# A transformer tower on one core: the last pair's end in two halves of the heads

## The chip, the core and the metric

The kernel runs on one core of a Trainium2 chip. The metric is device time in microseconds (us). PE is the matrix engine, DVE the vector engine, ACT the activation engine, POOL the general engine, and SP issues the DMAs. The five run their own streams in order and meet at semaphores.

## The reference

16 sequences of 512 tokens, 64 channels, all float32. In three steps:

```python
h = tok(ids)                                  # sines of 4 ids, two-layer MLP, layernorm, plus 0.1 * residual
h = h + attn(layernorm(h))                    # 8 heads of 64, one shared k and v; softmax; output product
h = h + ffn(layernorm(h))                     # router of 6 experts, top 2, three-layer experts
```

In the attention `ctx` of shape (b, 8, s, 64) is transposed over its heads and reshaped to (b, 512, s) before the output product with `Wo`, whose result is (b, s, 64). Written out, output token 64 h + d depends on head h alone (and on all tokens through its keys and values). So the tokens of a head can go through the last layernorm and the expert layer as soon as that head is done, whatever the others do.

## The kernel before, in words

**Pairs.** Two sequences make a pair, and there are 8 (`PAIRS`). A pair has 16 heads in all, taken two at a time (`a` = 0 to 7, `HH` = 8 such head pairs) and in quads of four (`QUADS` = 4). It is walked in 64 slots. A slot is one 128x512 tile of scores: its product on PE (L494, made for two slots at a time), its maximum on DVE (`maxima`, L899), its exponential on ACT (`exps`, L786, which also sums the row). Per 8 slots (one `a`) there are also the reciprocal of the sums (L905), the scaled output weights `woz` (`over_sums`, L349, on POOL; for the very last `a` on DVE), the product of the exponentials with them in two parts (`pv`, L525) and a block transpose into `m` on DVE (`turn`, L911). Per 16 slots one quad's queries are made (L506) and copied out (L792).

**What else runs beside the slots.** Beside pair i's scores run the token part of pair i+1 (`prep`) and the end of pair i-1 (`ffn`, `ffn_out`): the values' product FIN (`value_products`, L609), the addition to h (L1095), the layernorm (L916 to L939, with a power on POOL, L1204, and squares on ACT, L797), the transposes T (L535, copied out at L829), the router R and its logits L (L648, L659), the gating of 22 small DVE instructions in 7 parts (`gating`, L1029 to L1079), the experts E1 and E2 (L673, L684, copied out at L834, L1111 and L838), the last product Y in four blocks (L708), and the weighted sums of the outputs (L1126 on DVE, L358 to L371 on POOL).

**What sets the order.** Each engine's stream is written out by hand: for each slot the code issues the scores' instruction first and then whatever the tables say for that slot. `F` is the table for the ends of pairs 0 to 5, `Z` for pair 6 (which runs beside pair 7 and past it, slots 64 to 77) and `L` for pair 7 (after the last slot; `FIN0` is at slot 63). No queue is reordered. So a late wait on an engine holds back all that is behind it.

**The ring.** PSUM is a ring of four double banks (`RING`), and every product takes one (FIN takes two). `ring_order` lists the products in the order of PE's stream, `ring_places` gives each the bank whose last reader is earliest by the tables (`read_at`), and `free` makes PE wait for that reader.

**The last pair (table L).** FIN is in three parts (`fin_part`): FIN0 with all heads of the first sequence and the first four of the second, FIN1, and FIN2 with the two heads that come last. The rest of the end is on all 8 tiles of tokens: h, layernorm on DVE with POOL's power, 12 products of zeros (`warm`, L745) ahead of T, router, gating, E1, E2 (half of it copied by ACT), and four Y blocks, each weighted by DVE (`outputs`, L1137), with the sums in turn on POOL (even blocks) and DVE (odd blocks, L1141, L1144).

**Stores.** SP waits for the sums of a pair and stores it with two DMAs, one per sequence (L421 to L426).

## Time and profile before

| | us |
|---|---|
| median of 3 runs (705.65 to 707.96) | 707.37 |
| the profiled execution | 705.38 |
| its span, first to last instruction | 703.6 |
| PE busy | 650.5 (92%) |
| DVE busy | 546.5 (78%) |
| ACT busy | 470.0 (67%) |
| POOL busy | 277.9 (39%) |

Times below are counted from the start of the span. PE's busy time is that of the matmuls, whose ends are modelled; a row's start to the next row's start is the better price of one. In a timeline the columns are start, length, engine, line, operation, operands, count, and in brackets the idle time before it with what ended it.

### The profile page before, as it was taken

How to read it: one execution, taken by the hardware profiler on the slowest of the kernel's cores; microseconds unless marked ns; L12 is line 12 of the kernel's file. 1: busy time of each engine (PE TensorE's matmuls, PEld its weight loads, DVE VectorE, ACT ScalarE, POOL GpSimd, SP SyncE). 2: the span in 40 equal slices, each digit the busy share in tenths (PEclk: the TensorE clock that was granted, in tenths of full speed). 3: DMA queues.
4: the chain of work that ended last, by engine and by line, in shares of the span. 5: the costliest groups of instructions: out<-in, count | busy, mean ns of one | idle time of the engine just before them, and what ended most of it. 6: DMA issues, size and time to landing. Idle time of an engine off the chain costs nothing.

```text
span 703.6 us, 26738 instructions
## 1 busy us (share of the span) xinstructions
PE 650.5 (92%) x11632; PEld 370.6 (53%) x11632; DVE 546.5 (78%) x1078; ACT 470.0 (67%) x1183; POOL 277.9 (39%) x354
## 2 busy tenths in 40 slices
PE   5789999999999999999999999999999999999974
PEld 4445555445645465545654465454664446554652
DVE  5687878787797877878787887978878788687657
ACT  2678885975668665886658766687558866678321
POOL 1242215315652175502853146620764119211173
PEclk9899999999999999999999999999999999999999
DMA  4000000000000000000000000000000000000001
GB/s 164 1 3 3 1 3 3 3 2 2 18 2 2 2 3 18 2 2 2 17 5 2 2 3 18 2 2 2 3 18 2 2 2 3 18 2 3 3 2 32
DMA packets 9428, 6.66 MB, mean 9 GB/s; under 512 B 8672, under 2 KB 8800, under 8 KB 9184
## 3 DMA queue, kind: packets, MB, share of 16 engines
q1 hardware_dynamic: 9312, 4.97, 2.4%
q8 instruction: 91, 1.49, 0.9%
q14 instruction: 25, 0.20, 0.1%
HBM read 2.87 MB, written 2.10 MB: 7 GB/s over the span
## 4 chain that ended last, share of the span: by engine, by line
PE 60%; DVE 22%; ACT 7%; issue 6%; POOL 4%; DMA 0%; SPq 0%; DVEq 0%; ACTq 0%; POOLq 0%
PE s_bank L525 23%; PE s_bank L494 17%; DVE nmax L899 8%; ACT p L786 5%; PE s_bank L609 5%; DVE e2t L1111 3%; PE s_bank L684 3%; PE s_bank L673 2%; PE s_bank L506 2%; DVE st L916 2%; PE s_bank L708 1%; DVE hatt L1095 1%; PE s_bank L588 1%; PE s_bank L535 1%; ACT e1t L834 1%
## 5 line engine op out<-in xcount | busy, mean ns | idle before, releaser
L786 ACT ACTIVATE p<-s_bank,nmax 128x512 f32<-128x512 f32 x512 | 347.8, 691 | 146.9 <-DVE nmax L899 145.8
L899 DVE TENSOR_REDUCE nmax<-s_bank 128x1 f32<-128x512 f32 x512 | 325.5, 681 | 50.2 <-PE s_bank L494 49.6
L494 PE MATMUL s_bank<-kf,g 64*64 64x512 f32 x2048 | 260.9, 594 | 6.4 <-DVE y L1126 2.8
L525 PE MATMUL s_bank<-p,woz 64*64 64x256 f32 x4096 | 247.1, 377 | 10.0 <-POOL woz L349 4.4
L525 PEld LDWEIGHTS s_bank<-p,woz 64*64 64x64 f32 x4096 | 163.6, 133 | 124.8 <-issue 45.9
L349 POOL TENSOR_TENSOR woz<-cst,rz 128x256 f32<-128x256 f32 x126 | 74.6, 613 | 264.0 <-DVE rz L905 264.0
L494 PEld LDWEIGHTS s_bank<-kf,g 64*64 64x64 f32 x2048 | 74.2, 133 | 91.3 <-issue 48.1
L786 ACT ACTIVATION_READ_ACCUMULATOR p<-s_bank,nmax 128x1 f32 x512 | 105.3, 206 | 0.0
L911 DVE STREAM_TRANSPOSE m<-s_bank 128x512 f32<-128x512 f32 x64 | 45.6, 712 | 26.1 <-PE s_bank L525 26.1
L1204 POOL TENSOR_TENSOR st<-st,power 128x8 f32<-128x8 f32 x24 | 39.5, 1648 | 45.3 <-DVE st L926 45.3
L358 POOL TENSOR_TENSOR y<-y,gt 128x768 f32<-128x768 f32 x28 | 41.3, 1475 | 37.9 <-DVE gt L1079 20.7
L797 ACT ACTIVATE sq<-xc 128x512 f32<-128x512 f32 x24 | 15.0, 627 | 41.9 <-DVE xc L935 26.1
L1126 DVE TENSOR_TENSOR y<-s_bank,cst 128x768 f32<-128x768 f32 x28 | 26.7, 953 | 16.6 <-PE s_bank L708 10.2
L506 PE MATMUL s_bank<-kf,qk 64*64 64x512 f32 x256 | 33.9, 595 | 4.1 <-ACT p L786 3.1
L1111 DVE TENSOR_SCALAR e2t<-s_bank,cst 128x512 f32<-128x512 f32 x45 | 31.5, 745 | 5.7 <-PE s_bank L684 5.3
L708 PEld LDWEIGHTS s_bank<-cst,e2t 64*64 64x64 f32 x1536 | 27.5, 136 | 14.1 <-issue 10.7
L708 PE MATMUL s_bank<-cst,e2t 64*64 64x64 f32 x1536 | 28.2, 220 | 6.2 <-DVE e2t L1111 6.2
L366 POOL TENSOR_TENSOR ys<-y 128x384 f32<-128x384 f32 x30 | 30.0, 1001 | 9.0 <-DVE y L1137 6.8
L609 PE MATMUL s_bank<-m,v 32*64 32x256 f32 (+2 forms) x1152 | 31.9, 355 | 0.8 <-ACT p L786 0.6
L792 ACT COPY g<-s_bank 128x1024 f32<-128x1024 f32 x31 | 31.2, 1007 | 0.0
L609 PEld LDWEIGHTS s_bank<-m,v 32*64 32x64 f32 x1152 | 25.7, 131 | 7.7 <-issue 4.1
L834 ACT ACTIVATE e1t<-s_bank,cst 128x1024 f32<-128x1024 f32 x24 | 26.9, 1122 | 4.3 <-PE s_bank L673 4.1
(117 smaller groups left out, 501.6 us busy)
## 6 DMA issues: line engine op xcount, KB each, us to landing
tower_out<-o SPq DMA_DIRECT2D x16, 128.0 KB, 2.7
cst<-consts SPq DMA_DIRECT2D x1, 1070.0 KB, 8.1
e2t<-ids SPq DMA_DIRECT2D x1, 896.0 KB, 5.4
cst<-consts SPq DMA_DIRECT2D x1, 416.0 KB, 5.9
cst<-consts SPq DMA_DIRECT2D x1, 288.0 KB, 3.6
e2t<-ids SPq DMA_DIRECT2D x1, 128.0 KB, 2.9
cst<-consts SPq DMA_DIRECT2D x1, 3.0 KB, 1.7
```

The costliest lines, as they stand in the source:

```text
L349: ops.tensor_tensor(woz[:, kept, four, :].rearrange("q (m h) c -> q m h c", h=2), k("wo").rearrange("q (m c) -> q m c", m=4)[:, 2 * n:2 * ...
L358: ops.tensor_tensor(yt, yt, gt[:, 8, two, :].unsqueeze(3).to_broadcast([128, 2, NE, C]), ALU.mult).then_inc(y_pool, 1)
L494: last = pe.matmul(double[half(q), 512 * r:512 * r + 512], g[half(r), a // 2 % 2, a % 2, first:first + 64], kf[half(r), par, a // 4, :], s ...
L506: last = pe.matmul(double[half(q), 512 * r:512 * r + 512], qk[half(r), 2 * (quad % 2) + q, :], kf[half(r), par, quad // 2, :], start=True, ...
L525: last = pe.matmul(bank("PV", i, a)[half(q), 512 * hh:512 * hh + 256], woz[half(r), kept, 2 * mm + hh, :], keys[:, q, :, :], start=(part = ...
L609: last = pe.matmul(bank("FIN", i, s2)[half(b2), 512 * q + 32 * first:512 * q + 32 * end], v[quarter(g4), par, b2, n, :], m[quarter(g4), b2 ...
L708: last = pe.matmul(double[half(q), 512 * c + C * x:512 * c + C * x + C], e2t[half(c), x, first:first + 64], k("e3")[half(c), C * x:C * x + ...
L786: nc.scalar.activation(p[:, 8 * kept + c % 8, :], bank("S", i, c - r)[:, 512 * r:512 * r + 512], ACT.Exp, bias=nmax[:, c % 16:c % 16 + 1], ...
L899: nc.vector.tensor_reduce(nmax[:, c % 16:c % 16 + 1], bank("S", i, c - r)[:, 512 * r:512 * r + 512], AX.X, ALU.max, negate=True).then_inc( ...
L911: nc.vector.transpose(m[:, b2, n:n + 2, :, :].rearrange("q h n o -> q h (n o)"), bank("PV", i, a)[:, :].rearrange("q (h x) -> q h x", h=2) ...
L1111: last = nc.vector.tensor_scalar(e2t[:, 2 * e + r, :], bank("E2", i, e)[:, 512 * r:512 * r + 512], k("e2b")[:, 2 * e + r:2 * e + r + 1], 0 ...
L1204: nc.gpsimd.tensor_tensor(st[n][:, 4, :], st[n][:, 3, :], power[:, :], ALU.pow).then_inc(ln_step[n], 1)
```

## The change

The end of pair 7 is made in two halves. Table `L` goes. `LA` is the end of the first half: the heads 0 to 3 of both sequences, tiles 0 to 3, Y blocks 0 and 1. Its slots count from slot 32 of pair 7, so that it runs beside the second half of that pair's scores (its FIN is at slot 41, its Y at slot 63, its last output at slot 24 after the end). `LB` is the second half, and its slots count from slot 64. To have heads 0 to 3 of both sequences ready by slot 40, pair 7 takes its quads in the order 0, 2, 1, 3. FIN is in three parts again: heads 0 to 3 of both sequences; heads 4 to 7 of the first and 4, 5 of the second; heads 6, 7 of the second. All of LA's and LB's instructions work on four tiles, half as wide as before, so there are twice as many of them (except FIN, Y and the outputs, whose number stays).

Table `Z` is new from slot 16 on: pair 6's E1, E2 and Y come at slots 28 to 58 and its last output at slot 60, where they were at 44 to 77. The 12 products of zeros stay only in LB. The last pair is stored in two halves of the tiles, four DMAs where there were two. In all pairs a Y block now holds two neighbouring tiles (`2 * j, 2 * j + 1`, before `j, j + 4`), and x2 and the logits are laid out to match; the number and the sizes of those instructions are as before.

```diff
@@ -92,45 +92,90 @@
 Z = {'FIN': 11,
  'LN': 11,
  'SQ': 15,
- 'LN2': 16,
- 'T': 22,
- 'T_ACT': 20,
- 'R': 23,
- 'R_ACT': 23,
- 'L': 24,
- 'GATE': (26, 26, 29, 31, 36, 42, 43),
- 'GATE_ACT': (25, 36),
- 'E1': (44, 47, 54),
- 'E1_ACT': (45, 47, 54),
- 'E2': (59, 62, 63),
- 'E2_DVE': (58, 64, 66),
- 'Y': (65, 72, 75, 77),
- 'Y_DVE': (69, 71, 74, 77)}
-L = {'FIN0': 63,
- 'FIN1': 0,
- 'FIN2': 9,
- 'LN': 7,
- 'SQ': 0,
- 'LN2': 8,
- 'T': 12,
- 'T_ACT': 9,
- 'R': 13,
- 'R_ACT': 9,
+ 'LN2': 18,
+ 'T': 23,
+ 'T_ACT': 23,
+ 'R': 24,
+ 'R_ACT': 24,
+ 'L': 26,
+ 'GATE': (26, 28, 28, 29, 33, 38, 41),
+ 'GATE_ACT': (25, 37),
+ 'E1': (28, 33, 38),
+ 'E1_ACT': (29, 33, 39),
+ 'E2': (34, 39, 40),
+ 'E2_DVE': (37, 39, 40),
+ 'Y': (46, 49, 52, 58),
+ 'Y_DVE': (46, 47, 53, 60)}
+LA = {'FIN': 9,
+ 'LN': 9,
+ 'SQ': 9,
+ 'LN2': 12,
+ 'T': 17,
+ 'T_ACT': 15,
+ 'R': 17,
+ 'R_ACT': 16,
+ 'L': 21,
+ 'GATE': (21, 22, 24, 24, 26, 31, 32),
+ 'GATE_ACT': (21, 28),
+ 'E1': (19, 22, 25),
+ 'E1_ACT': (19, 22, 24),
+ 'E2': (25, 26, 28),
+ 'E2_ACT': (23, 25, 27),
+ 'E2_DVE': (24, 26, 30),
+ 'Y': (31, 31),
+ 'Y_DVE': (35, 56)}
+LB = {'FIN': 9,
+ 'FIN2': 15,
+ 'LN': 11,
+ 'SQ': 9,
+ 'LN2': 19,
+ 'T': 18,
+ 'T_ACT': 18,
+ 'R': 18,
+ 'R_ACT': 26,
  'L': 28,
- 'GATE': (14, 24, 31, 31, 31, 37, 61),
- 'GATE_ACT': (18, 32),
- 'E1': (23, 42, 45),
- 'E1_ACT': (15, 19, 24),
- 'E2': (43, 50, 55),
- 'E2_ACT': (28, 39, 53),
- 'E2_DVE': (35, 35, 35),
- 'Y': (57, 60, 62, 63),
- 'Y_DVE': (61, 62, 63, 63)}
+ 'GATE': (27, 28, 29, 33, 35, 40, 57),
+ 'GATE_ACT': (28, 56),
+ 'E1': (25, 36, 38),
+ 'E1_ACT': (28, 32, 37),
+ 'E2': (39, 39, 48),
+ 'E2_ACT': (38, 54, 63),
+ 'E2_DVE': (34, 37, 39),
+ 'Y': (61, 63),
+ 'Y_DVE': (61, 63)}
+PARTS = ((LA, SLOTS // 2), (LB, SLOTS))
+def real_quad(i, quad):
+    return (0, 2, 1, 3)[quad] if i == PAIRS - 1 else quad
+def real_pair(i, a):
+    return 2 * real_quad(i, a // 2) + a % 2
+def last_parts(slot):
+    for n, (table, first) in enumerate(PARTS):
+        if 0 <= slot - first < SLOTS:
+            yield table, PAIRS - 1 + n, slot - first
+def outputs_of(f):
+    return (0, 1) if f is LA else (2, 3) if f is LB else (0, 1, 2, 3)
...
+            if i + 1 == PAIRS:
+                for table, index, own in last_parts(slot):
+                    ffn(index, own, table)
...
+    f, first = F if i + 2 < PAIRS else Z, SLOTS * (i + 1)
+    if i + 1 >= PAIRS:
+        n = e // 2 if name == "Y" else i + 1 - PAIRS
+        f, first, e = PARTS[n][0], SLOTS * (PAIRS - 1) + PARTS[n][1], e % 2 if name == "Y" else e
...
+        def part_of(f):
+            js = outputs_of(f)
+            first, end = js[0], js[-1] + 1
+            return js, slice(2 * first, 2 * end), slice(128 * first, 128 * end), len(js) == 2
...
-            yt, two = y[:, j % 2, :, :, :], slice(j, 8, 4)
+            yt, two = y[:, j % 2, :, :, :], slice(2 * j, 2 * j + 2)
...
-            def store(i, last=False):
-                sp.wait_ge(y_pool, 4 * W_SUM * i + (2 * W_LAST if last else 4 * W_SUM))
-                if last:
-                    sp.wait_ge(y_dve, 4)
+            def store(i, tiles):
                 for b2 in range(2):
                     dst = out[2 * i + b2, :, :].rearrange("(h d) c -> d h c", d=KD)
-                    sp.dma_start(dst, o[64 * b2:64 * b2 + 64, :, :]).then_inc(stored, 16)
-            for n in range(PAIRS):
-                store(n, n == PAIRS - 1)
-            sp.wait_ge(stored, 32 * PAIRS)
+                    sp.dma_start(dst[:, tiles, :], o[64 * b2:64 * b2 + 64, tiles, :]).then_inc(stored, 16)
+            for n in range(PAIRS - 1):
+                sp.wait_ge(y_pool, 4 * W_SUM * (n + 1))
+                store(n, slice(0, 8))
+            for part in range(2):
+                sp.wait_ge(y_pool, 4 * W_SUM * (PAIRS - 1) + W_LAST * (part + 1))
+                sp.wait_ge(y_dve, 2 * part + 2)
+                store(PAIRS - 1, slice(4 * part, 4 * part + 4))
+            sp.wait_ge(stored, 32 * (PAIRS + 1))
...
+                heads = real_quad(i, quad)
                 for r in range(2):
                     for q in range(2):
-                        last = pe.matmul(double[half(q), 512 * r:512 * r + 512], qk[half(r), 2 * (quad % 2) + q, :],
-                                         kf[half(r), par, quad // 2, :], start=True, stop=True)
+                        last = pe.matmul(double[half(q), 512 * r:512 * r + 512], qk[half(r), 2 * (heads % 2) + q, :],
+                                         kf[half(r), par, heads // 2, :], start=True, stop=True)
...
-                i, par = PAIRS - 1, (PAIRS - 1) % 2
-                pe.wait_ge(mtd, HH * i + HH - 2 + n)
-                if n == 0:
-                    free("FIN", i, 0)
-                    free("FIN", i, 1)
-                value_products(i, par, *(((0, 0, 8), (1, 0, 4)), ((1, 4, 6),), ((1, 6, 8),))[n]).then_inc(fin_parts, 1)
+                i, index, par = PAIRS - 1, PAIRS - 1 + min(n, 1), (PAIRS - 1) % 2
+                pe.wait_ge(mtd, HH * i + (HH // 2, HH - 1, HH)[n])
+                if n < 2:
+                    free("FIN", index, 0)
+                    free("FIN", index, 1)
+                heads = (((0, 0, 4), (1, 0, 4)), ((0, 4, 8), (1, 4, 6)), ((1, 6, 8),))[n]
+                value_products(index, par, *heads).then_inc(fin_parts, 1)
...
+                if slot == f["FIN"]:
+                    if ends:
+                        fin_part(i + 1 - PAIRS)
+                    else:
+                        pe.wait_ge(mtd, HH * i + HH)
+                        free("FIN", i, 0)
+                        free("FIN", i, 1)
+                        value_products(i, par, (0, 0, HEADS), (1, 0, HEADS)).then_inc(fin_ps, 1)
+                if f is LB and slot == f["FIN2"]:
+                    fin_part(2)
...
+                    if f is LB:
                         pe.wait_ge(ln_dve[2], LN_DVE * i + 1)
                         free("XT", i)
                         warm(WARM_T, bank("XT", i))
                     pe.wait_ge(ln_step[2], LN_STEP[2] * i + 3)
...
+                                last = pe.matmul(double[half(q), 512 * r:512 * r + count],
+                                                 k("e1")[half(r), first:first + 64], xt[half(r), cols],
...
+                    if not nxt:
+                        for table, index, own in last_parts(slot):
+                            ffn(index, par, own, table)
+                            ffn_out(index, own, table)
...
+                b2, n = real_pair(i, a) // 4, 2 * (real_pair(i, a) % 4)
...
+                    wait(dve, y_pool, 4 * W_SUM * min(i, PAIRS - 1))
...
+                    if ends:
+                        dve.wait_ge(fin_parts, 1 if f is LA else 3)
...
+                pair = PAIRS - 1
                 dve.wait_ge(gated, i + 1)
-                dve.wait_ge(y_pool, 4 * W_SUM * i + (W_LAST if j == 2 else 0))
+                dve.wait_ge(y_pool, 4 * W_SUM * pair + (W_LAST if j == 2 else 0))
...
-                    dve.wait_ge(stored, 32 * i)
+                    dve.wait_ge(stored, 32 * pair)
...
-                ffn(PAIRS - 1, 1, slot, L)
+                for table, index, own in last_parts(slot + SLOTS):
+                    ffn(index, 1, own, table)
```

The rest of the diff passes `tiles`, `cols` and `count` of `part_of(f)` to the layernorm, the gating and the copies, so that they take those of their half, and calls `last_parts` in the streams of ACT, DVE and POOL as in PE's.

## Rows read from the trace of the kernel before

**Rows 1.** The page's first part: busy time and share.
```profile
PE 650.5 (92%) x11632; PEld 370.6 (53%) x11632; DVE 546.5 (78%) x1078; ACT 470.0 (67%) x1183; POOL 277.9 (39%) x354
```

**Rows 2.** Busy time by stretch: start and end, length, engines, clock, DMA.
```profile
587.40:624.30 36.90, 35.22 (x601) 20.87 (x605) 27.65 (x55) 25.34 (x69) 16.55 (x23) 1.00 0.04 10
624.30:655.50 31.20, 30.82 (x399) 15.01 (x395) 25.86 (x55) 24.66 (x65) 4.73 (x8) 1.00 0.01 2
655.50:671.60 16.10, 15.24 (x476) 10.98 (x472) 8.13 (x14) 2.37 (x8) 4.05 (x6) 1.00 0.01 3
671.60:703.60 32.00, 18.75 (x464) 11.81 (x462) 21.33 (x46) 7.31 (x11) 17.81 (x24) 0.90 0.08 18
```

**Rows 3.** PE's timeline around the last scores.
```profile
654.62 1.04 PE L494 MATMUL s_bank<-kf,g 64*64 64x512 f32 x8
...
656.34 1.91 PE L525 MATMUL s_bank<-p,woz 64*64 64x256 f32 x32
...
659.13 4.75 PE L609 MATMUL s_bank<-m,v 32*64 32x256 f32 x192
663.81 0.93 PE L708 MATMUL s_bank<-cst,e2t 64*64 64x64 f32 x48
664.56 1.04 PE L525 MATMUL s_bank<-p,woz 64*64 64x256 f32 x15
666.23 3.31 PE L525 MATMUL s_bank<-p,woz 64*64 64x256 f32 x49 [0.64 <-issue]
...
670.38 1.16 PE L609 MATMUL s_bank<-m,v 32*64 32x64 f32 x64
```

**Rows 4.** DVE's timeline, FIN and a Y block of pair 6.
```profile
601.51 0.75 DVE L1095 TENSOR_TENSOR hatt<-h,s_bank 128x256 f32<-128x256 f32 x2 [3.64 <-PE s_bank L609]
...
664.80 0.96 DVE L1126 TENSOR_TENSOR y<-s_bank,cst 128x768 f32<-128x768 f32 x1 [2.26 <-PE s_bank L708]
```

**Rows 5.** The chain that ended last: start, length, what.
```profile
671.60 1.42 DVE h L1095 x4
...
676.63 1.66 POOL st L1204
...
679.06 0.69 PE s_bank L535 x32
679.76 1.04 PE s_bank L708 x48
680.80 0.85 PE s_bank L648 x8
681.65 1.73 PE s_bank L673 x8
```

**Rows 6.** DVE's timeline: gating, outputs, end.
```profile
683.89 0.21 DVE L1029 TENSOR_REDUCE gs<-s_bank 128x8 f32<-128x48 f32 x1 [2.08 <-PE s_bank L659]
...
685.75 0.80 DVE L1043 TENSOR_TENSOR gt<-gt,gs 128x48 f32<-128x48 f32 x1
...
688.98 2.06 DVE L1111 TENSOR_SCALAR e2t<-s_bank,cst 128x512 f32<-128x512 f32 x3
...
691.08 0.17 DVE L1068 TENSOR_SCALAR gs<-gs 128x8 f32<-128x8 f32 x1
...
692.37 2.02 DVE L1137 TENSOR_TENSOR y<-s_bank,gt 128x768 f32<-128x768 f32 x2
...
699.54 0.31 DVE L1144 TENSOR_TENSOR o<-ys,h 128x128 f32<-128x128 f32 x1
```

**Rows 7.** The page's DMA issues: KB each, us to landing.
```profile
tower_out<-o SPq DMA_DIRECT2D x16, 128.0 KB, 2.7
...
cst<-consts SPq DMA_DIRECT2D x1, 3.0 KB, 1.7
```

**Rows 8.** Busy time by stretch after the transposes, for PE's clock.
```profile
679.00:681.00 2.00, 1.94 (x86) 1.78 (x90) 1.03 (x3) 0.58 (x1) 1.05 (x1) 0.73 0.03 8
681.00:683.50 2.50, 2.50 (x38) 1.13 (x32) 0.81 (x1) 0.78 (x2) 2.29 (x4) 0.53 0.00 0
```

More of the change, by code:

```diff
@@ L153, in ffn @@
     def ffn(i, slot, f):
-        if f is not L and slot == f["FIN"]:
+        if slot == f["FIN"]:
             order.extend([("FIN", i, 0), ("FIN", i, 1)])
@@ L163, in ffn @@
                 order.append(("E2", i, e))
-        for j in range(4):
-            if slot == f["Y"][j]:
-                order.append(("Y", i, j))
+        for n, j in enumerate(outputs_of(f)):
+            if slot == f["Y"][n]:
+                order.append(("Y", min(i, PAIRS - 1), j))
     for slot in range(SLOTS):
@@ L191, in ring_order @@
                 ffn(i - 1, slot, F if i + 1 < PAIRS else Z)
-            if i + 1 == PAIRS and slot == L["FIN0"]:
-                order.extend([("FIN", i, 0), ("FIN", i, 1)])
+            if i + 1 == PAIRS:
+                for table, index, own in last_parts(slot):
+                    ffn(index, own, table)
     for slot in range(SLOTS):
@@ L198, in ring_order @@
         ffn(PAIRS - 2, slot + SLOTS, Z)
-        ffn(PAIRS - 1, slot, L)
+        for table, index, own in last_parts(slot + SLOTS):
+            ffn(index, own, table)
     return order
@@ L682, in ffn @@
                             for c in range(2):
[L683 to L684 removed]
+                                first, from_col = e * 128 + 64 * r, 512 * c + cols.start
+                                last = pe.matmul(double[half(c), 512 * r:512 * r + count],
                                                  k("e2")[half(r), first:first + 64],
[L686 removed]
+                                                 e1t[half(r), e, from_col:from_col + count], start=True, stop=True)
                         last.then_inc(e2_ps, 1)
             def ffn_out(i, slot, f=F):
[L690 to L694 removed]
+                js, tiles, cols, ends = part_of(f)
+                for n, j in enumerate(js):
+                    if slot == f["Y"][n]:
+                        pair = min(i, PAIRS - 1)
+                        free("Y", pair, j)
+                        double = bank("Y", pair, j)
+                        if ends:
                             for c in range(2):
@@ L773, in _ @@
                 ffn_out(PAIRS - 2, slot + SLOTS, Z)
-                ffn(PAIRS - 1, 1, slot, L)
-                ffn_out(PAIRS - 1, slot, L)
+                for table, index, own in last_parts(slot + SLOTS):
+                    ffn(index, 1, own, table)
+                    ffn_out(index, own, table)
         @block.scalar
@@ L867, in body @@
                         ffn(i - 1, slot, F if nxt else Z)
+                    if not nxt:
+                        for table, index, own in last_parts(slot):
+                            ffn(index, own, table)
             def sines(n):
@@ L890, in _ @@
                 ffn(PAIRS - 2, slot + SLOTS, Z)
-                ffn(PAIRS - 1, slot, L)
+                for table, index, own in last_parts(slot + SLOTS):
+                    ffn(index, own, table)
         @block.vector
@@ L1116, in ffn @@
                     if slot == f["GATE"][part]:
-                        gating(i, part)
-                for j in range(4):
-                    if slot == f["Y_DVE"][j]:
-                        dve.wait_ge(y_ps, 4 * i + j + 1)
-                        src = bank("Y", i, j)[:, :].rearrange("q (t c) -> q t c", t=2)[:, :, 0:NE * C]
-                        if f is L:
+                        gating(i, part, f)
+                for n, j in enumerate(js):
+                    if slot == f["Y_DVE"][n]:
+                        pair = min(i, PAIRS - 1)
+                        dve.wait_ge(y_ps, 4 * pair + j + 1)
+                        src = bank("Y", pair, j)[:, :].rearrange("q (t c) -> q t c", t=2)[:, :, 0:NE * C]
+                        if ends:
                             outputs(i, j, src.rearrange("q t (e c) -> q t e c", e=NE))
@@ L1160, in body @@
                         ffn(i - 1, 1 - par, slot, F if nxt else Z)
+                    if not nxt:
+                        for table, index, own in last_parts(slot):
+                            ffn(index, par, own, table)
             dve.wait_ge(load_four, 16)
@@ L1188, in _ @@
                 ffn(PAIRS - 2, 0, slot + SLOTS, Z)
-                ffn(PAIRS - 1, 1, slot, L)
+                for table, index, own in last_parts(slot + SLOTS):
+                    ffn(index, 1, own, table)
         @block.gpsimd
@@ L1255, in body @@
                         ffn(i - 1, slot, F if nxt else Z)
+                    if not nxt:
+                        for table, index, own in last_parts(slot):
+                            ffn(index, own, table)
             nc.gpsimd.memset(spare[:, :], 0.0).then_inc(spare_set, 1)
@@ L1270, in _ @@
                 ffn(PAIRS - 2, slot + SLOTS, Z)
-                ffn(PAIRS - 1, slot, L, True)
+                for table, index, own in last_parts(slot + SLOTS):
+                    ffn(index, own, table)
 def laid_out(x):
```

202 lines of the change are left out of this document (95 added, 107 removed).

## The prediction

> **What bounds the kernel now.** I read the page first, then the busy time by stretch of the last pair and of what follows it, then PE's timeline at the end of the scores, DVE's timeline, and the chain that ended last. The page shows PE busy for 92% of the span [rows 1]. The stretches split the part that the change touches [rows 2]. The first half of pair 7's slots (587.4 to 624.3) has PE busy 35.2 of 36.9 us, the second half (624.3 to 655.5) 30.8 of 31.2: both are PE's, and DVE has 9.2 and 5.3 us to spare. From the end of the last scores to the end of FIN (655.5 to 671.6) PE is busy 15.2 of 16.1. In the last 32.0 us no engine is busy for more than two thirds: this is a chain of single instructions. So the change trades PE time in a full stretch against idle time in an empty one. What counts is how much more the second half of the slots takes, and by how much the two stretches behind it shrink. Three runs before have a median of 707.37; the profiled execution took 705.38 with a span of 703.6. I make the sum on the span and put the difference on the median. A measurement of this kernel can tell 0.3% (2.1 us) from no change.
>
> **Term 1: the slots get longer.** Prices on PE: 0.86 for a product like the scores' (two from 654.62 to 656.34), 0.75 for a Y block (663.81 to 664.56), 4.7 for FIN0 and FIN1 together, of which FIN1, like FIN2, is 1.1, so 3.6 for a FIN that is 256 columns wide and 1.8 for the new first part with 128 [rows 3]. In the first half of the slots one E1 of pair 6 comes in: +0.9. In the second half pair 6 loses that E1 (-0.9) and gets two E2 (+1.7) and four Y (+3.0) that lay behind the last scores; the first half of the heads brings its FIN (1.8), six halves of E1 and E2 (6 x 0.43 = 2.6), and T, R and L (about 0.9, half of what the chain has for T and R and as much again [rows 5]). Together 9.1: PE's 30.8 become 39.9.
> DVE in the same stretch: 25.9 now. Pair 6's third gating part goes ahead of it (-1.3, it ran beside POOL), two more pairs of e2t copies (4 x 0.66 = 2.6, from three in 2.06 [rows 6]) and four Y additions (4 x 0.9 = 3.6 [rows 4]) come in. From the first half of the heads come: four additions to h at 0.25 and a layernorm of about 1.8; 17 gating instructions at 0.235 (4.0); three e2t copies at 0.37 (1.1). Sum 38.7. The two engines are then as good as equally full, and each waits for the other. In the first half of the slots, where PE idles 1.7 of 36.9 (4.6%), DVE is 75% full [rows 2]; the same share of 39.9 would be 1.8 lost. With DVE at over 90% I take 2.4, and as bounds 0 and 9 (below). The stretch is 42.3 long instead of 31.2. The last scores end 0.9 + 11.1 = **12.0 us later**, at 667.5.
> ACT has 24.7 busy and gets some 6: covered. POOL gets pair 6's four sums (4 us each) and one power. They stand in front of `woz`, and the worst bunch (slots 46 to 55) is 13.2 us of POOL's against about 12 of slots, with `woz` wanted five slots later: nothing, and 1 to 2 us if the sums come later than their slots. Before, these sums lay beside an idle end.
>
> **Term 2: from the last scores to the end of FIN.** Now 16.1. After: the rest of the second-last products (1.7 [rows 3]); the first half's two Y blocks (2 x 1.4: 0.75, and 0.65 for the bias of 384 columns); the last pair of heads, 3.5 if it costs 2 x 1.73 and 5.0 as it did (664.56 to 669.54, with 0.64 of "issue") [rows 3], I take 4.2; the second FIN part 1.8, beside which DVE's last transpose is hidden; the third 1.2. Sum 11.7: **4.4 us less**. It is less because FIN0, Y of pair 6 and an E2 have gone ahead. The last reciprocal and `woz` on DVE come ahead of the first half's last gating parts in DVE's stream, so these hold up nobody but the first half's own output; that output waits for pair 6's stores too, and only POOL's sum and the second last store stand behind it.
>
> **Term 3: the last 32.0 us, on half the tiles.**
> - To the last layernorm step (671.6 to 679.06): additions to h 1.42, now 1.0 (a 128x128 addition is 0.31 [rows 6], a 128x256 one 0.36 [rows 5]); six DVE and ACT steps and the squares, 4.4 together, of which 0.2 each is fixed (0.17 for 128x8 [rows 6]) and the rest halves: 2.9; POOL's power 1.66 [rows 5]. No row has it on 4 columns: between 0.83 and 1.66, I take 1.1, nearer to the half, since 8 elements cost ten times a plain small operation.
> - T to the logits (679.06 to 683.89, 4.8): about half, 2.6. Pair 6's Y, which stood between T and R [rows 5], is gone.
> - Gating (683.89 to 692.37, 8.5): e2t 2.06 becomes 1.1; 22 instructions at 0.24 (5.2) become 4.7, for 128x48 takes 0.21 and 128x8 0.17; 1.2 over goes, which is DVE slowed while POOL made pair 6's sums (0.80 for L1043 [rows 6], whose like take 0.21); 0.4 stays for the exponential's round trip. The first half's second output (2.8, a quarter of 7.5 plus a sum) is put on DVE between the layernorm and this gating, where 2.6 is free: +0.4. Sum 6.6.
> - Outputs 692.37 to 699.85: 7.5 for four blocks, 3.75 for two.
> - Last sum to the end: 3.75. A store of 128 KB lands in 2.7, one of 3 KB in 1.7 [rows 7]; so the half lies between 2.75 and 3.75, and I take 3.6.
> Sum 21.5: **10.5 us less**, bounds 19.5 and 24.
> The Trainium skill ("DMA: Bandwidth & Descriptors", the table of two cost components) gives a DMA about 2.0 us fixed and its bytes over 436e9 per second. By that a store of 64 KB would end 0.15 before one of 128, so the last term would be 3.6 also, and the stores in halves would be worth next to nothing.
>
> **Covered.** The new places of tiles in Y, x2 and logits: same counts and sizes in every pair. The other order of quads: only indices. Two more DMAs on SP, which waits anyway: its second last pair of stores needs the first half's sums, some 15 us before the end. WARM_T remains in front of T and now ends about 0.5 us ahead of it.
>
> **Sum.** 12.0 - 4.4 - 10.5 = **-2.9**: span 700.7, and 704.5 on the median.
>
> **Rivals.**
> *DVE becomes the bound, with its waits (slower).* DVE's stream is strict, so a wait for PE holds back the maxima of the scores. Rows for such waits: 3.64 for a FIN, during which only two banks are left to the scores [rows 4]; 2.08 for logits [rows 6]; 2.26 for a Y block [rows 4], of which I take half for each of four. With 10.2 of idle on 38.7 of work the second half of the slots takes 48.9, 6.6 above my 42.3: 12.0 + 6.6 - 4.4 - 10.5 = +3.7, 711.1. It decides from 47.3 (8.6 us idle) on. For it: the two sums are equal. Against it: now DVE idles there mostly because PE is late, and some of the waits would fall into PE's share.
> *The half-sized end runs at the lower clock (no change).* After the idle time before the transposes PE's granted clock falls to 0.73 and 0.53 [rows 8], its level of 1.2 GHz, and an E1 takes 1.73 instead of 0.86 [rows 5]. The new end has shorter matmuls with gaps of their own; at that level all through, its E2 and two Y blocks cost some 2 us more: -0.9, 706.5. Against it: the idle stretch before T shrinks from 2.3 to about 0.5.
> The Trainium skill ("TensorE: Matmul & The Clock Gate", the two states) says that an idle PE falls back to 1.2 GHz until it has been kept busy; the trace agrees.
> *It all fits (more).* No loss in the slots and no gap in the last heads' product: -2.4 and -0.7 more: -6.0, 701.4. For it: the second half now loses only 0.4.
>
> **How the numbers follow.** Forecast 0.46, DVE bound 0.21, lower clock 0.18, all fits 0.15. Faster by over 0.3% is the first and the last: 0.61; the same 0.18; slower 0.21. The forecast's own range is 701.5 to 707. The whole range reaches down past "all fits" by half the bounds of term 3, to 699.5, and up to 710.0, which leaves out most of the slower rival's upper half.
>
> **What would show it.** The last score product ends near 667.5 (12 us later) and the second half of the slots lasts about 42; PE is busy 94% there, DVE over 90%. FIN ends 11.7 later, the rest takes 21.5. Slower if that half lasts over 47, with DVE idle behind FIN, logits and Y of the first half. I am wrong about the end if from FIN's end on it still takes over 24, by a power that doesn't shrink or matmuls at 1.2 GHz; wrong about POOL if PE waits for `woz` at slots 52 or 60.

## The result and the profile after

The changed kernel has a median of 704.64 us in 20 runs (702.99 to 706.34), the kernel before 707.02 in 20 runs (704.82 to 708.05). The ratio is 0.9968, with an interval of 0.9958 to 0.9978: 2.4 us faster, just above the 0.3% that the prediction set as what can be told. The forecast was 2.9 us and 704.5. One execution in one of the experiments below (12 early, second output early) took 852.06 at a granted clock of 0.75 and stays out of its ratio.

The runs of the changed kernel lie in two groups. Nine are between 703.0 and 703.7, with a mean granted clock of PE of 0.990 to 0.993; eight are between 705.4 and 706.3, with 0.986 or 0.987; three lie between. The execution that was profiled took 705.7, so it is of the upper group, and its span of 703.9 is no shorter than that of the profile before. The kernel before spreads too: five of its 20 runs are between 704.8 and 705.9, fifteen between 706.5 and 708.1, and its profiled execution (705.38) is like the five. So these two traces together show 0.3 us more where the 20 runs each show 2.4 less. The gain is told by the medians and the ratio; the traces tell what single steps cost. No trace of the lower group of the changed kernel was kept.

Busy time by stretch, of the kernel after, cut where its own last score product and its own FIN end (start:end, length, PE, PE's weight loads, DVE, ACT, POOL, granted clock, DMA):

```profile
587.91:625.19 37.28, 36.04 (x609) 20.79 (x613) 28.40 (x58) 26.10 (x69) 16.57 (x23) 1.00 0.04 10
625.19:668.71 43.52, 41.42 (x812) 22.07 (x808) 37.75 (x88) 28.48 (x75) 17.83 (x25) 1.00 0.01 3
668.71:681.34 12.63, 11.43 (x404) 8.35 (x396) 6.04 (x16) 2.74 (x9) 5.26 (x9) 1.00 0.11 25
681.34:703.90 22.56, 13.15 (x224) 9.61 (x224) 14.05 (x43) 4.58 (x11) 3.33 (x5) 0.82 0.06 13
```

Against [rows 2] the slots take 80.8 us instead of 68.1, the way to the end of FIN 12.6 instead of 16.1, and the rest 22.6 instead of 32.0. Pair 7 also begins 0.5 later (587.91 against 587.37). The change doesn't touch what lies before it; the granted clock was lower in the start-up (a mean of 0.65 instead of 0.72 from 10 to 20 us). Over all 14 traces pair 7 begins between 587.2 and 588.4, so this alone moves an execution by up to 1.2 us.

PE's timeline of the kernel after, from the last score product on (start, length, engine, line, operation, operands, count, idle time before it and what ended it), to set beside [rows 3]:

```profile
667.85 1.07 PE L550 MATMUL s_bank<-kf,g 64*64 64x512 f32 x8
668.74 1.91 PE L582 MATMUL s_bank<-p,woz 64*64 64x256 f32 x32
...
673.16 3.96 PE L582 MATMUL s_bank<-p,woz 64*64 64x256 f32 x64
677.04 2.74 PE L666 MATMUL s_bank<-m,v 32*64 32x128 f32 x178
680.85 0.45 PE L666 MATMUL s_bank<-m,v 32*64 32x64 f32 x14 [1.07 <-issue]
682.75 5.49 PE L812 MATMUL s_bank<-spare 128*128 128x128 f32 x24 [1.45 <-DVE st L992]
688.17 0.71 PE L592 MATMUL s_bank<-cst,x 64*64 64x64 f32 x16
```

Two things are new. The second and third part of FIN (together 192 matmuls) stop after 178 of them, and PE stands for 1.07 us that the profile puts on nothing ("issue"). And the 24 matmuls on zeros (12 products of `warm`) take 5.49 us, where they took 2.94 before. The transposes behind them start at 688.17. DVE had written their input by 686.0. The zeros in PE's timeline of the kernel before:

```profile
673.79 2.94 PE L745 MATMUL s_bank<-spare 128*128 128x128 f32 x24 [1.40 <-DVE st L916]
```

DVE's timeline of the kernel after, in the order of [rows 6]:

```profile
685.60 0.42 DVE L1015 TENSOR_TENSOR x<-xc,st 128x256 f32<-128x256 f32 x1 [1.13 <-POOL st L1289]
...
690.90 0.18 DVE L1106 TENSOR_REDUCE gs<-s_bank 128x4 f32<-128x24 f32 x1 [2.18 <-PE s_bank L722]
...
696.80 2.03 DVE L1218 TENSOR_TENSOR y<-s_bank,gt 128x768 f32<-128x768 f32 x2
...
700.35 0.29 DVE L1225 TENSOR_TENSOR o<-ys,h 128x128 f32<-128x128 f32 x1
```

PE's granted clock around the zeros, by stretches of 1 us of the same trace (columns as above):

```profile
681.00:682.00 1.00, 0.31 (x14) 0.17 (x10) 0.64 (x4) 0.00 (x0) 0.00 (x0) 1.00 0.00 0
682.00:683.00 1.00, 0.25 (x1) 0.25 (x2) 0.90 (x5) 0.00 (x0) 0.00 (x0) 0.54 0.06 16
683.00:684.00 1.00, 1.00 (x6) 1.00 (x7) 0.52 (x2) 0.42 (x1) 0.00 (x0) 0.50 0.00 0
...
688.00:689.00 1.00, 0.88 (x18) 0.52 (x16) 0.69 (x2) 0.05 (x1) 0.00 (x0) 0.54 0.00 0
689.00:690.00 1.00, 0.63 (x16) 0.43 (x16) 0.00 (x0) 0.43 (x2) 0.00 (x0) 1.00 0.00 0
```

After the standing in FIN and the idle time before the zeros, the clock is at 0.5, the level of 1.2 GHz, and stays there until the zeros are over. They were put there to lift the clock. They ran at half of it, nearly twice as long as planned, and held back what they should have helped. That is 2.2 us (688.17 less 686.0), and the two groups of runs are some 2.5 apart. That this is what parts the groups is likely, not shown. There are also states between: in two kernels below with the same zeros at the same place (the last pair stored whole, and three parts all behind the transpose) the clock came back up while the zeros ran; they took 4.57, and the transposes started 1.2 us after their input was there.

```profile
682.69 4.57 PE L811 MATMUL s_bank<-spare 128*128 128x128 f32 x24 [1.45 <-DVE st L991]
```

This row is PE's, of the kernel that stores the last pair whole.

### The profile page after: what moved, and what is told of

It is laid out like the page before. It is cut to its first block, busy times and chain, and to the rows that moved or that the text cites. A ratio compares the mean times of both kernels' runs of the same rounds, so it can differ in the third digit from the quotient of the medians.

```text
span 703.9 us, 27039 instructions
## 1 busy us (share of the span) xinstructions
PE 654.0 (93%) x11752; PEld 374.2 (53%) x11752; DVE 549.9 (78%) x1114; ACT 472.2 (67%) x1194; POOL 277.7 (39%) x355
## 4 chain that ended last, share of the span: by engine, by line
PE 67%; DVE 19%; ACT 6%; issue 4%; POOL 3%; DVEq 0%; POOLq 0%
PE s_bank L582 25%; PE s_bank L550 20%; DVE nmax L975 7%; PE s_bank L666 4%; ACT p L854 4%; DVE e2t L1190 3%; PE s_bank L736 3%; PE s_bank L747 3%; PE s_bank L563 2%; PE s_bank L773 2%; PE s_bank L812 2%; DVE st L992 2%; DVE hatt L1174 1%; PE s_bank L645 1%; PE s_bank L592 1%
## 5 line engine op out<-in xcount | busy, mean ns | idle before, releaser
L1289 POOL TENSOR_TENSOR st<-st,power 128x8 f32<-128x8 f32 (+1 forms) x25 | 39.9, 1596 | 59.1 <-DVE st L1002 59.1
L865 ACT ACTIVATE sq<-xc 128x512 f32<-128x512 f32 (+1 forms) x25 | 15.3, 610 | 38.3 <-DVE xc L1011 22.5
L1190 DVE TENSOR_SCALAR e2t<-s_bank,cst 128x512 f32<-128x512 f32 (+1 forms) x48 | 32.3, 712 | 5.8 <-PE s_bank L747 5.3
L904 ACT ACTIVATE e1t<-s_bank,cst 128x1024 f32<-128x1024 f32 (+1 forms) x27 | 27.5, 1024 | 2.0 <-PE s_bank L736 2.0
```

The source lines that it names most:

```text
L1190: last = nc.vector.tensor_scalar(e2t[:, 2 * e + r, cols], bank("E2", i, e)[:, 512 * r:512 * r + count], k("e2b")[:, 2 * e + r:2 * e + r + ...
L1289: nc.gpsimd.tensor_tensor(st[n][:, 4, tiles], st[n][:, 3, tiles], power[:, tiles], ALU.pow).then_inc(ln_step[n], 1)
```

## The experiments

All medians are against the kernel before on the same chip in the same hour; the ratio is what compares them. It is formed from all the runs and need not be the quotient of two medians. In those hours the kernel before had medians from 706.52 to 707.77, so two medians of this table can differ by some 1 us more or less than the kernels do.

| kernel | median | ratio | interval |
|---|---|---|---|
| changed | 704.64 | 0.9968 | 0.9958 to 0.9978 |
| only table Z (in the kernel before) | 706.98 | 1.0002 | 0.9992 to 1.0011 |
| first half 8 slots later | 710.63 | 1.0064 | 1.0045 to 1.0083 |
| last pair stored whole | 705.21 | 0.9985 | 0.9973 to 0.9998 |
| no zeros | 704.98 | 0.9971 | 0.9960 to 0.9981 |
| 5 of zeros | 704.06 | 0.9962 | 0.9950 to 0.9975 |
| 12 of zeros, early | 703.57 | 0.9956 | 0.9941 to 0.9971 |
| 18 of zeros, early | 703.59 | 0.9958 | 0.9945 to 0.9972 |
| 12 early, second output early | 703.65 | 0.9954 | 0.9941 to 0.9967 |
| 20 of zeros in the kernel before | 707.05 | 1.0006 | 0.9997 to 1.0015 |
| one FIN behind the last transpose | 702.04 | 0.9930 | 0.9918 to 0.9942 |
| one FIN, 12 early | 702.82 | 0.9934 | 0.9922 to 0.9947 |
| three parts, all behind the transpose | 705.53 | 0.9974 | 0.9961 to 0.9988 |

### Which part of the change brings it

The first kernel is the one before with the new table `Z` from slot 16 on and nothing else.

```diff
- 'E1': (44, 47, 54), ... 'E2': (59, 62, 63), ... 'Y': (65, 72, 75, 77),
+ 'E1': (28, 33, 38), ... 'E2': (34, 39, 40), ... 'Y': (46, 49, 52, 58),
```

> The kernel before with nothing changed but table Z (pair 6's E1, E2 and Y earlier). By the ledger of the prediction: the slots get 4.7 us longer (E1 +0.9 in the first half; -0.9, two E2 1.7, four Y 3.0 in the second) and some 0.3 of loss; the stretch to the end of FIN gets 2.5 shorter (two E2 and a Y); the last 32.0 get 1.6 shorter (1.2 of DVE slowed beside POOL, 0.4 of a Y in front of R). Sum +0.9, so 707.9 against 707.0. Rival: the early E2 and Y were what the change gained by (they fill idle time of PE in the slots): -1.5 or more, and the two halves bring little.

The ratio is 1.0002. The rival's gain is not there. The small loss of 0.9 that was expected is at the edge of the interval and can't be told from nothing. Its busy time by stretch, cut at its own ends:

```profile
587.80:625.00 37.20, 35.95 (x608) 20.74 (x612) 28.40 (x58) 26.02 (x68) 16.58 (x23) 1.00 0.04 10
625.00:662.60 37.60, 35.37 (x600) 18.21 (x595) 31.31 (x60) 25.17 (x68) 17.45 (x25) 1.00 0.01 3
662.60:675.87 13.27, 11.70 (x356) 8.82 (x348) 3.57 (x7) 1.45 (x4) 2.32 (x4) 1.00 0.10 22
675.87:705.10 29.23, 17.57 (x368) 11.31 (x368) 18.00 (x44) 7.35 (x11) 6.30 (x9) 0.89 0.05 11
```

The slots take 6.7 more than before (expected 5.0), the way to the end of FIN 2.8 less (2.5), the last stretch 2.8 less (1.6). Of the last, 1.6 is where pair 6's sums no longer run on POOL beside DVE: the gating takes 7.2 instead of 8.5, the centring of 128x512 takes 0.69 instead of 0.99, and the comparison that took 0.80 [rows 6] takes 0.21. The other 1.2 lies between the transposes and the logits (3.6 instead of 4.8), where pair 6's Y block is gone and the first E1 ran at full clock, for which only 0.4 was expected. What the slots lost above the expectation is in large part in PE's timeline:

```profile
650.86 1.96 PE L527 MATMUL s_bank<-p,woz 64*64 64x256 f32 x32 [1.05 <-ACT p L788]
...
659.99 1.96 PE L527 MATMUL s_bank<-p,woz 64*64 64x256 f32 x32 [0.61 <-POOL woz L351]
```

The second is the wait for `woz` behind POOL's sums that the prediction named as possible. In the changed kernel's trace it isn't there; that this is because its slots are longer is likely, not shown. So moving pair 6's end forward is worth nothing by itself, within the 0.1% of the interval. That it makes room for the halves is argued only: the halves with the old table Z weren't tried.

The next kernel has the first half's end 8 slots later.

```diff
-PARTS = ((LA, SLOTS // 2), (LB, SLOTS))
+PARTS = ((LA, SLOTS // 2 + 8), (LB, SLOTS))
```

> The changed kernel with the first half's end 8 slots later (it begins at slot 40). Its gating, E1 to E2 and Y then lie behind the last scores. If the slots are full and the time is simply moved: the last scores end 3 to 4 us earlier and FIN that much later, so within 1 us of the changed kernel. If the overlap is worth something (work of PE that hides DVE's chain): 2 to 5 us slower, for DVE's 5 us of gating then stand in front of the last transpose. If DVE in the slots is the bound now: faster by 1 to 2 us.

It is 6 us slower than the changed kernel by the medians and 6.8 by the ratios. The overlap is worth that, but the way is not quite as expected. Four of the six runs are between 709.8 and 710.7, two at 713.2 and 713.8; the profiled one is the slowest (713.81, a span of 712.0). PE's timeline of this kernel:

```profile
649.08 2.08 PE L666 MATMUL s_bank<-m,v 32*64 32x128 f32 x128 [1.17 <-DVE y L1206]
...
668.00 1.07 PE L550 MATMUL s_bank<-kf,g 64*64 64x512 f32 x8
...
684.50 0.46 PE L666 MATMUL s_bank<-m,v 32*64 32x64 f32 x15 [1.71 <-issue]
686.41 5.49 PE L812 MATMUL s_bank<-spare 128*128 128x128 f32 x24 [1.45 <-DVE st L992]
```

The last score product ends at 668.9, 80.8 after the pair's begin at 588.1: just as late as in the changed kernel, not 3 to 4 us earlier, though there is less work among the slots. Work was taken out, and waits came in (1.17 here in front of FIN, others of 0.4 to 0.8). FIN then ends 16.1 after the scores instead of 12.6. And the first half's second output now lies in the middle of the second half's gating, as DVE's timeline shows:

```profile
696.31 0.18 DVE L1122 TENSOR_TENSOR gt<-gt,cst 128x24 f32<-128x24 f32 x1
696.42 0.96 DVE L1218 TENSOR_TENSOR y<-s_bank,gt 128x768 f32<-128x768 f32 x1
...
698.94 0.29 DVE L1225 TENSOR_TENSOR o<-ys,h 128x128 f32<-128x128 f32 x1
```

That costs 2.7 on the chain. The span of this trace is 8.1 longer than that of the changed kernel's. Of that, 3.5 are the way to FIN, 2.7 this output, and nearly 2 the last products of E2 and Y, which ran at a granted clock of 0.5 here (699.4 to 706.2) and which the outputs on DVE had to wait for. The last part may be what the four faster runs don't have; no trace of them was kept.

The third kernel stores the last pair whole.

```diff
-            for part in range(2):
-                sp.wait_ge(y_pool, 4 * W_SUM * (PAIRS - 1) + W_LAST * (part + 1))
-                sp.wait_ge(y_dve, 2 * part + 2)
-                store(PAIRS - 1, slice(4 * part, 4 * part + 4))
+            sp.wait_ge(y_pool, 4 * W_SUM * (PAIRS - 1) + 2 * W_LAST)
+            sp.wait_ge(y_dve, 4)
+            store(PAIRS - 1, slice(0, 8))
```

> The changed kernel with the last pair stored whole, by two DMAs of 128 KB at the end instead of four of 64 KB. The half store lands in 2.2 us against 2.8: 0.3 to 0.6 slower than the changed kernel. Rival (the landing is all fixed cost): no difference, within 0.1.

It is 0.6 slower by the medians, near the upper end of what was expected, but the intervals of the two overlap, and its runs are also in two groups (704.2 to 705.3, 706.1 to 707.4). The traces are clearer than the medians. From the last two stores' issue to the end there are 3.7 us here (699.50 to 703.2), 3.2 in the changed kernel (700.72 to 703.9). The page of the changed kernel has the same difference in its landings (KB each, median us to landing):

```profile
tower_out<-o SPq DMA_DIRECT2D x14, 128.0 KB, 2.8
...
tower_out<-o SPq DMA_DIRECT2D x4, 64.0 KB, 2.2
```

### The zeros and the clock

Four kernels change `warm` ahead of the second half's transposes: none, 5, and 12 or 18 that start right behind FIN.

```diff
-WARM0, WARM, WARM_T = 14, 10, 12
+WARM0, WARM, WARM_T = 14, 10, 0
```

```diff
                     if f is LB:
-                        pe.wait_ge(ln_dve[2], LN_DVE * i + 1)
                         free("XT", i)
                         warm(WARM_T, bank("XT", i))
```

> The changed kernel without the 12 products of zeros ahead of the last transposes. Theory A (in the profiled run they ran at 1.2 GHz, took 5.5 us instead of 2.9 and held the transposes back by 2.3 us; in about half the runs this is so): the slow group of runs near 705.7 goes, and the transposes start about 0.05 after x is written (at 686.0 instead of 688.2), but all products after them run at 1.2 GHz for some us, which costs about 1 to 2 us, so the median is 703.5 to 705. Theory B (the products of zeros earn more than they cost in every run): 705.5 to 707, all runs.

> 5 products of zeros, where they are now. At 1.2 GHz they take 2.3 us and end at 685.1, before x is ready at 686.0, so they can hold nothing back. Theory A: the group near 705.7 goes and the median is 703.3 to 704. Theory B (fewer of them leave the transposes and experts at 1.2 GHz): the median is 704.5 to 705.5.

> The changed kernel with the 12 products of zeros right behind the last part of FIN, without their wait for the layernorm's mean (only for the bank). Theory A (the clock falls in the 1.4 us that PE idles between FIN and these products): they begin near 681.9 instead of 682.75, at 2.4 GHz more often, and are over at 684.9; the runs near 705.7 become rare and the median is 703 to 703.5. Theory B (the clock has fallen for what PE did before, so that an earlier start changes nothing but its time): still two groups of runs, 2.3 us apart, the upper one 0.9 us lower.

> As the early 12, but 18 of them, which at 2.4 GHz end about 4.4 us after they begin, at 686.3, just when x is ready. Theory A: median 703.0 to 703.5 with the transposes and what follows at 2.4 GHz. Theory B (two levels by chance): where they run at 1.2 GHz they end 8.8 us after they begin, at 690.7, and the upper group of runs is near 708.

Without zeros there are no two groups any more: 11 runs from 704.0 to 705.5. PE's timeline and the clock by stretch of that kernel:

```profile
686.94 0.70 PE L592 MATMUL s_bank<-cst,x 64*64 64x64 f32 x16 [4.98 <-DVE x L1015]
...
688.60 1.08 PE L736 MATMUL s_bank<-xt,cst 64*64 64x256 f32 x8
...
689.87 1.97 PE L736 MATMUL s_bank<-xt,cst 64*64 64x256 f32 x16
```

```profile
690.00:692.00 2.00, 2.00 (x24) 1.14 (x24) 1.41 (x8) 1.44 (x4) 0.00 (x0) 0.50 0.28 66
692.00:694.00 2.00, 2.00 (x32) 1.12 (x24) 1.73 (x11) 1.53 (x3) 0.00 (x0) 0.76 0.00 0
```

The transposes follow x at once, but E1 and E2 run at half speed (two E1 take 1.97 instead of 1.07). Both prices are about 2 us: the zeros at 1.2 GHz (2.2 above), and going without (this trace's span is 1.9 longer than that of the early 12 below). With 5, the median is 704.06, a little above the range of theory A. Its trace agrees with both theories in part: the zeros' 2.5 us at the low level are over before x comes, but they don't lift the clock, and two E1 take 1.97 there too.

The early 12 begin as soon as FIN is over instead of 1.45 us later:

```profile
680.57 0.45 PE L666 MATMUL s_bank<-m,v 32*64 32x64 f32 x14 [1.07 <-issue]
680.95 2.94 PE L811 MATMUL s_bank<-spare 128*128 128x128 f32 x24
685.80 0.46 PE L592 MATMUL s_bank<-cst,x 64*64 64x64 f32 x16 [1.90 <-DVE x L1014]
```

They take 2.94, the clock reads 1.00 from 680 to 698, and no run of six is above 704.3. Theory A of that run holds, though the median (703.57) is 0.07 outside its range. 18 of them bring no more, and two of nine runs are above 705. The ratios of these two and the changed kernel are 0.9956, 0.9958 and 0.9968; the intervals overlap, so that about 1 us was gained is shown by the traces and the groups of runs more than by the ratio.

> The early 12 products of zeros, and the first half's second output on DVE at slot 40 of its own (behind the last transpose, while FIN runs) instead of slot 56 (between the layernorm and the gating of the second half). With the early 12 this output ends at 688.4 and the logits come at 688.2: 0.2 to 0.5 faster than the early 12 alone if it holds back the gating, no difference (within 0.1) if it does not. 0.3 slower if it holds back the last additions to h.

The edit is `'Y_DVE': (35, 56)` to `(35, 40)`. There is no difference: 0.9954. That output was covered. Its trace is also a warning on the early 12: they took 2.94, PE idled 1.89 as before, and this time the clock fell at 688.7, so that two E1 took 1.69. In all four traces with the zeros early they ran at the full level themselves; what came behind them did not always.

> The kernel before with 20 products of zeros instead of 12 at the same place. In its profile the 12 end at 676.7, PE idles 2.3 us and the granted clock is 0.5 when R and the first E1 run (1.73 us instead of 0.86). Theory A (the clock in the last stretch is worth as much there): 20 end at 678.7, T to the logits takes 1.0 to 1.5 us less, median 705.5 to 706.2; so a part of what the change brings could be had without it. Theory B (where the 20 themselves run at 1.2 GHz they end at 683.6, 4.6 late): two groups, median 707 to 709.

The kernel before with `WARM_T = 20` is not faster: 1.0006. The zeros do what they should, the first E1 takes 1.04 (at 681.70) instead of 1.95 in the same view of the kernel before (1.73 on the chain [rows 5]), and the logits come 0.4 earlier although pair 7 began 0.7 later in this trace. But then DVE's gating meets POOL's sums of pair 6: one step of 128x48 takes 1.52 instead of 0.32 in the kernel before, beside a POOL instruction of 1.47 that starts with it. The copies behind the gating are what Y waits for, PE idles 2.85, and the last products run at the low level. PE's timeline of that kernel:

```profile
674.55 4.73 PE L745 MATMUL s_bank<-spare 128*128 128x128 f32 x40 [1.40 <-DVE st L916]
...
681.70 1.04 PE L673 MATMUL s_bank<-xt,cst 64*64 64x512 f32 x8
...
691.87 1.03 PE L708 MATMUL s_bank<-cst,e2t 64*64 64x64 f32 x48 [2.85 <-DVE e2t L1111]
692.67 1.51 PE L698 MATMUL s_bank<-cst 64*64 64x384 f32 x8
```

So eight more zeros did not bring there what the change brings. Other numbers of them weren't tried.

### The standing in FIN

In all nine traces with FIN in three parts, PE stands near the end of the second and third part's 192 matmul records, for 1.07 to 1.84 us: after 178 of them in eight, after 177 in the kernel with the first half 8 slots later. This kernel makes the two parts one, behind the last transpose:

```diff
-                pe.wait_ge(mtd, HH * i + (HH // 2, HH - 1, HH)[n])
+                pe.wait_ge(mtd, HH * i + (HH // 2, HH)[n])
...
-                heads = (((0, 0, 4), (1, 0, 4)), ((0, 4, 8), (1, 4, 6)), ((1, 6, 8),))[n]
+                heads = (((0, 0, 4), (1, 0, 4)), ((0, 4, 8), (1, 4, 8)))[n]
...
-                if f is LB and slot == f["FIN2"]:
-                    fin_part(2)
...
-                        dve.wait_ge(fin_parts, 1 if f is LA else 3)
+                        dve.wait_ge(fin_parts, 1 if f is LA else 2)
```

> The changed kernel with the second and third part of FIN made as one behind the last transpose: 64 products of two matmuls each instead of 96, the same columns, but begun 0.8 us later. In the changed kernel PE stands 1.07 to 1.84 us in the middle of these parts for nothing that the profile shows. Theory A (many short instructions in a row outrun the supply of instructions): with a third less of them the standing goes or shrinks, FIN ends 1.0 to 1.6 us earlier, and the median is 703.0 to 703.7. Theory B (it is something else that comes at that time, or the place in the program): FIN ends no earlier, or later by 0.1 to 0.8, since its start waits for the transpose.

The median is 702.04, better than theory A's range (the kernel before was at 706.52 in that hour, 0.5 lower than beside the changed one): 0.9930 against 0.9968, with intervals that do not meet. PE's timeline:

```profile
677.96 2.09 PE L666 MATMUL s_bank<-m,v 32*64 32x128 f32 x128 [0.84 <-DVE m L985]
681.48 2.94 PE L810 MATMUL s_bank<-spare 128*128 128x128 f32 x24 [1.43 <-DVE st L990]
684.80 0.46 PE L592 MATMUL s_bank<-cst,x 64*64 64x64 f32 x16 [0.38 <-DVE x L1013]
```

FIN waits 0.84 for the transpose and still ends at 680.05, where it ended at 681.34. Two things make that up: the standing of 1.07 is gone, and the same columns in 128 matmuls take 2.09 where the 192 took 3.19; against them stands a start 0.9 later. And the zeros, at their old place behind the same idle time of 1.43, run at 2.4 GHz: the clock reads 1.00 up to 699, and the five runs lie between 701.5 and 702.3 with a clock of 0.992 to 0.994. The 1.3 us of FIN and the half of the runs that lost 2.3 us by the zeros (1.2 on the mean) make 2.5; 2.6 was measured. The 1.2 rests on the reading of the two groups that the result section calls likely.

> One FIN behind the last transpose, and the 12 products of zeros right behind it without their wait. If both causes are right and add up: 1.0 to 1.6 below the kernel with the early 12 alone, so 702.0 to 702.6 by the median, and no group of runs 2.3 above it. If the standing is not cured by it: 703.5.

The two do not add up: 702.82 against 702.04, with overlapping intervals. Here the zeros end at 683.2, PE idles 1.9 us until x is there, and in the profiled run the clock fell at the end of T (a mean of 0.71 from 685 to 687, 0.50 from 687 to 689; two E1 took 1.77). Two of its five runs were at 701.5, three at 702.8.

> The changed kernel with the second part of FIN made to wait for the last transpose (as the one FIN did), but still in two parts of 64 and 32 products, one behind the other. It tells what cured the standing. Theory A1 (the number of short instructions behind each other, 96 products instead of 64): the standing of 1 us or more is back, FIN ends near 682 and the median is 704.5 to 706. Theory A2 (the pause of 0.8 us ahead of FIN lets the supply catch up): no standing, FIN ends near 681.0, the products of zeros run at 2.4 GHz, and the median is 702.8 to 703.3.

This kernel only changes the wait: `(HH // 2, HH - 1, HH)` to `(HH // 2, HH, HH)`. PE's timeline:

```profile
677.22 2.73 PE L666 MATMUL s_bank<-m,v 32*64 32x128 f32 x178 [0.84 <-DVE m L987]
681.37 0.45 PE L666 MATMUL s_bank<-m,v 32*64 32x64 f32 x14 [1.41 <-issue]
683.27 4.57 PE L812 MATMUL s_bank<-spare 128*128 128x128 f32 x24 [1.45 <-DVE st L992]
```

The pause in front of FIN is there, and the standing too, at the same record. So it is not the pause that cured it (A2 falls), and the median is 705.53. It went with the 64 matmuls that are no longer there. Whether their number counts, or that the same place of the program now lies behind FIN, where PE waits anyway, these runs can't tell. The number alone is not enough: in the kernel before the 192 matmuls of FIN0 and FIN1 went through in 4.75 us without a stop [rows 3], one in 25 ns, where the 178 here take 15 ns each, and PE stood only 0.64, behind 48 more and 15 of the next product.

The traces have one thing more that bears on it. Among the DMA queues of the page is one named "instruction", which moves 16 KB at a time. The stretches of the changed kernel around one of its transfers (PE is in FIN):

```profile
678.25:678.50 0.25, 0.25 (x37) 0.25 (x28) 0.00 (x0) 0.00 (x0) 0.19 (x1) 1.00 0.26 66
678.50:679.50 1.00, 1.00 (x87) 1.00 (x80) 0.00 (x0) 0.00 (x0) 0.46 (x1) 1.00 0.00 0
```

The transfer is recorded from 678.40 to 679.45, and PE goes on at 680.85. In each of the nine traces PE goes on 1.2 to 1.6 us after the end of such a transfer, however long it stood, and in the kernel before it goes on 1.4 after one (664.84 and 666.23). In the kernel with one FIN the transfer is recorded from 679.52 to 680.78, so it ends after FIN is over. Other transfers of this queue pass without a standing. So it is likely that PE waits there for its instructions. No run changed that alone, so it is not shown.

## Why the prediction was right

**Term 1 (12.0 later).** Measured 12.7 from the pair's own start. PE's work in the second half of the slots was 41.4 where I summed 39.9: its idle time was 2.1 where I took 2.4, and DVE's work 37.8 where I summed 38.7. So DVE's sum held, and so did the loss, which was a guess between bounds of 0 and 9: that it hit is in part luck. PE's added work was sized too small, 10.6 where I had 9.1, and makes the miss of 1.2 (43.5 against 42.3). Rows for it: an E1 half that starts at 651.84 took 0.67, not 0.43, and the first part of FIN 2.03 (637.48 to 639.51), not 1.8; they are not a full account. In the first half of the slots the E1 that came in cost 0.4 instead of 0.9, for it fell partly into idle time.

**Term 2 (4.4 less).** Measured 3.5 less. The last heads' product took 3.9 (I took 4.2); the standing that was in it before [rows 3] is in FIN now, and costs 1.07 instead of 0.64. I had counted it with the product that it hit, as if it belonged there. Without it the second and third part of FIN took 3.2 where I took 3.0.

**Term 3 (10.5 less).** Measured 9.4 less in the profiled run, and by steps: additions to h 0.9 (1.0), layernorm with the power 3.7 (4.0; the power on 4 columns is 1.02 where I took 1.1, between the bounds of 0.83 and 1.66), T to the logits 2.7 (2.6), gating 5.9 (6.6), outputs 3.8 (3.75), the end 3.3 (3.6). That makes 20.3. The 2.2 above it are the zeros at 1.2 GHz. The power's row, POOL's:

```profile
684.55 1.02 POOL L1289 TENSOR_TENSOR st<-st,power 128x4 f32<-128x4 f32 x1 [5.57 <-DVE st L1002]
```

Without the 2.2 these terms would put the changed kernel 2.5 us below the profiled execution before (705.38), and with pair 7's later begin at 703.4: where its lower group is.

**The rivals.** DVE did not become the bound: it was busy 87% of the second half of the slots (I had said over 90%) and its waits for PE were short (1.43 at most in front of a Y). The clock was, as the rival had it, what the sum lacked; but the step where it struck was wrong. I placed it in E2 and Y, at 2 us in all runs, and took the zeros as "now ends about 0.5 us ahead of" T. They ended 2.2 behind x in the profiled run. The upper group (705.4 to 706.3) is near the 706.5 of that rival, though not by its mechanism; the lower (703.0 to 703.7) lies between the forecast and "it all fits" (701.4), nearer to the forecast.

That the median came out within 0.2 us of 704.5 is in part luck. Three things hide behind it. The forecast was set off from a median of three runs, 707.37; 20 runs gave 707.02, and the gain was 2.4 where 2.9 was forecast. The median of 704.64 lies between two groups, where only three of 20 runs are. And the errors of the terms offset each other: term 1 cost 0.7 more than forecast and term 2 saved 0.9 less, while term 3 without the zeros' delay saved 1.2 more. With that delay in half of the runs, which no term had, the terms would give a gain of some 1.4 only; the rest to 2.4 they don't explain. They were summed on a profiled execution of the kernel before that was 1.6 faster than its median, and no trace shows what its slower runs lose. The mechanism holds: each of the three terms came within 1.2 us of its forecast.

The Trainium skill ("DMA: Bandwidth & Descriptors", the two cost components) gave 0.15 us between a store of 64 and one of 128 KB; the traces have 0.5 to 0.6 and decide. The page's table stands under the DMAs that GpSimd issues, and these are SP's. My own lower bound for that step was no better founded: the row of 3 KB [rows 7] is a load of constants, not a store.

## What to carry to other kernels

When an empty chain at the end is shortened by moving work into full stretches, add up each engine's work there first, then what the chain's own steps cost at half the size. Here, in the profiled executions, 12.7 us were paid for 12.9. With margins as thin as that, the small instructions' fixed cost and the clock decide the sign.

Products of zeros that hold the clock up are work on the path whenever the clock has fallen already: ask what they cost at the low level, and who is behind them. Of what was tried, the one FIN, with no standing ahead of the zeros, did best: 2.94 in its trace, and five runs within 0.7 us. Their number mattered less.

Splitting a product so that a part can start 0.9 us earlier is not free if it makes more short instructions. The unsplit one began later and ended 1.3 us earlier.

## What the runs showed of the hardware

- PE stood for 0.64 to 1.84 us with no wait in sight, in or behind a run of many short matmuls, in the kernel before and in each of the nine traces with FIN in three parts. In those nine it stood after 178 of 192 records of FIN (once after 177), and its length changed from trace to trace (1.07 to 1.84). With 128 records instead of 192 it was gone. In all ten, PE went on 1.2 to 1.6 us after the recorded end of a 16 KB transfer of the queue named "instruction".
- 24 matmuls of 128x128 on zeros took 2.94 at a granted clock of 1.00, 5.49 at 0.50, and 4.57 where the clock rose while they ran, in six traces all behind idle time of 1.40 to 1.45 us. What lay further ahead differed: 1.07 us or more of standing in FIN in the four slower ones, none in FIN in the two others. Whether that decides it isn't shown.
- DVE steps on 48 elements took up to 0.80 us (1.52 in the kernel with 20 zeros) while POOL worked on its sums, and 0.21 when it didn't. A 128x512 addition took 0.99 and 0.69.
- POOL's power took 1.65 us on 8 columns and 1.02 on 4; a DVE step on 24 elements took 0.18, on 48 0.21, so that halving the gating saved a tenth.
